# Holding back two gathers of old key blocks until the second attention group's rows have landed, in a one-core four-layer kernel

## What is computed

```
k_blocks = k_blocks.at[blk, :, off, :].set(k)     # 64 x 32 new keys go into the cache
v_blocks = v_blocks.at[blk, :, off, :].set(v)
k_all = k_blocks[block_tables] ...                # rows of each entry's window
scores = einsum(qg, k_all) * SCALE                # masked to a window of 128 positions
p = softmax(scores)
o = einsum(p, v_all) ; out = einsum(o, Wo)
```

## Time and profile before

| what | us |
|---|---|
| runs before | 958.57, 965.36, 964.55; median 964.55 |
| the profiled execution | 957.4, of it span 955.3 |
| attention, start of the keys of the first and of the last entry | 459.08 and 597.5 |

### The profile page before, as it was taken

How to read it: one execution, slowest core, us unless ns; L and a number is a source line. 1 busy time by engine, 2 the same in 40 slices (tenths; PEclk the granted TensorE clock), 3 DMA queues, 4 the chain that set the end, 5 groups by cost and what they waited for, 6 DMA issues and landing times.

```text
span 955.3 us, 16539 instructions
## 1 busy us (share of the span) xinstructions
PE 832.4 (87%) x5239; PEld 674.2 (71%) x5239; DVE 567.7 (59%) x1659; ACT 347.7 (36%) x1007; POOL 381.1 (40%) x405
## 2 busy tenths in 40 slices
PE   1999998976899998785489799979979979999997
PEld 1787776754798997674378687877447747777786
DVE  5656888655587886289288799451553434444343
ACT  3333443433233332112277788402442222221311
POOL 7300436367566676766545540000175003434000
PEclk9999999996999999898599999959999979999999
DMA  9226111787977551924888876000523003331232
GB/s 353 67 89 177 47 44 63 295 252 215 247 212 229 159 139 38 348 78 121 159 166 172 160 168 218 2 1 1 187 101 123 24 17 93 104 104 57 89 82 94
DMA packets 68179, 126.43 MB, mean 132 GB/s; under 512 B 20224, under 2 KB 50265, under 8 KB 65455
## 3 DMA queue, kind: packets, MB, share of 16 engines
q1 hardware_dynamic: 46783, 75.49, 26.3%
q0 software_dynamic: 20800, 47.76, 18.1%
q10 hardware_dynamic: 512, 2.13, 1.0%
HBM read 87.39 MB, written 43.30 MB: 137 GB/s over the span
## 4 chain that ended last, share of the span: by engine, by line
PE 59%; DMA 13%; DVE 10%; issue 5%; SPq 5%; ACT 4%; POOL 3%; DVEq 0%; POOLq 0%; ACTq 0%
PE ps L470 18%; PE ps L807 10%; PE ps L838 7%; SPq L1097 3%; PE ps L817 3%; DMA early<-newblk,new_i 2%; DMA early<-early 2%; PE ps L2277 2%; DMA big<-mid 2%; PE ps L828 2%; DMA mid<-sent_d 2%; PE ps L2514 2%; PE ps L2293 2%; PE ps L2559 1%; POOL sent_d L909 1%
## 5 line engine op out<-in xcount | busy, mean ns | idle before, releaser
L909 POOL DMA_INDIRECT sent_d<-mid,slot_i x88 | 98.3, 1117 | 111.1 <-DVE mid L629 65.2
L851 ACT ACTIVATE early<-ps 128x256 f32<-128x256 f32 x134 | 51.5, 384 | 175.0 <-PE ps L817 173.3
L838 PE MATMUL ps<-early 96*128 (+1 forms) x346 | 97.5, 382 | 0.2
L869 DVE TENSOR_TENSOR early<-early,ps 128x96 f32<-128x96 f32 (+1 forms) x134 | 37.3, 278 | 96.0 <-ACT early L857 80.1
L900 POOL DMA_INDIRECT back_d<-early,mid x78 | 77.1, 989 | 35.1 <-issue 29.9
L504 DVE TENSOR_TENSOR hidl<-work,hidh 128x512 fp32r<-128x512 f32 (+1 forms) x56 | 38.8, 693 | 84.4 <-ACT hidh L497 84.4
L807 PE MATMUL ps<-big,early 128*128 x380 | 81.2, 337 | 3.6 <-issue 2.0
L900 POOL DMA_INDIRECT back_d<-big,mid x39 | 38.4, 985 | 112.6 <-DVE big L883 106.7
L510 ACT ACTIVATE work<-ps 128x512 f32<-128x512 f32 (+1 forms) x56 | 33.4, 596 | 136.4 <-PE ps L470 136.2
L807 PEld LDWEIGHTS ps<-big,early 128*128 128x128 f32 x380 | 68.8, 196 | 10.4 <-issue 5.4
L807 PE MATMUL ps<-early 128*128 x156 | 56.0, 482 | 4.6 <-ACT early L851 4.4
(11 more groups left out here) (440 smaller groups left out, 2094.3 us busy)
## 6 DMA issues: line engine op xcount, KB each, us to landing
mid<-sent_d SPq DMA_DIRECT2D x117, 130.0 KB
big<-back_d SPq DMA_DIRECT2D x8, 512.0 KB
mid<-back_d SPq DMA_DIRECT2D x8, 512.0 KB, 6.4
early<-back_d SPq DMA_DIRECT2D x16, 256.0 KB, 3.1
early<-in_w SPq DMA_DIRECT2D x3, 1024.0 KB, 11.9
big<-in_gate SPq DMA_DIRECT2D x1, 3072.0 KB, 10.7
big<-in_up SPq DMA_DIRECT2D x1, 3072.0 KB, 15.8
early<-in_gu SPq DMA_DIRECT2D x1, 2816.0 KB, 10.6
```

What stands on the lines that cost most here:

```text
L838: last = nc.tensor.matmul(ps[:, 6 + j % 2, 0:D], L.hTb[j % len(L.hTb)][0:f1 - f0, h * P:(h + 1) * P], L.down[0:f1 - f0, h, bass.ds(owners[ ...
L851: nc.scalar.activation(L.yTb[b % ring_y], ps[:, b % 2, 0:2 * P], ACT.Copy).then_inc(s["turn_sb"], 1)
L869: nc.vector.tensor_tensor(L.hb[j % ring_h], L.sgb[j % 2], ps[:, 2 + j % 2, F:2 * F], ALU.mult)\
L909: nc.gpsimd.indirect_dma_start(out=sent_d, out_offset=bass.IndirectOffsetOnAxis(ap=L.slot_i[:, i:i + 1], axis=0), in_=L.rows[c][:, t, n, : ...
```

## The change

In the part written out by hand, GpSimd issues the gather of group 4 not between the turns of groups 1 and 2 but behind the turn of group 2, and it waits there until SyncE's half of the turn of group 1 has landed. The turn of group 3 moves up, ahead of the gather of group 5. All transfers stay the same.

```diff
             turn_rows(1)
-            old_rows(4)
             pool.wait_ge(s["qkv_end"], 1)
             nc.gpsimd.memset(pickw, 0.0).then_inc(s["qzero"], 1)
             turn_rows(2)
+            pool.wait_ge(s["into1"], turned(1))
+            old_rows(4)
+            turn_rows(3)
             old_rows(5)
             new_rows(4)
             old_rows(6)
-            turn_rows(3)
             new_rows(5)
             old_rows(7)
             for g in range(6, NT):
```

## The result

The changed kernel takes 965.95 us (median of 20 runs, 960.50 to 971.63) against 961.81 us of the kernel before (20 runs, 957.35 to 967.37). The ratio is 1.004, with a 95% interval of 1.0021 to 1.006: about 4 us or 0.4% slower, as forecast, though less than the 1% that the prediction took as what a measurement can tell from no change. The execution profiled after took 961.96 us.

What follows compares the result with a forecast made beforehand. The prediction took the chain of turns and new rows up to group 11's landing as the bound. Group 1's gain 0, rows' delay +4.0, rest 0, on the 964.55 us median: 968.5 us, range 957.5 to 978.

Steps and rivals of the forecast that it cites:

- What bounds the kernel: Attention: a chain of turns and new rows up to group 11's landing; TensorE's 7.58 us wait before group 1 off it.
- The rows of group 1: SyncE's last issue to landing: 5 us instead of 11.5, TensorE starting group 1 some 6.5 us sooner, worth nothing by itself.
- The gather of group 4: GpSimd: issued 10.7 us later, 8 us from it to new rows 4, which go 7.5 us later.
- New rows 6: GpSimd: the gather of group 6 ends last instead of the turn of group 2; 3.5 us delay on this path.
- SyncE's turns: SyncE's queue: turn 4 at 487.1 instead of 479.53; turn 6 late by 3.5 to 5.8 us, taken as 4.0.
- From there to group 11: Later rounds of the loop: the delay is handed on at the same 33 us a round, no change counted.
- signs of being wrong: Group 1 landing after 472, new rows 6 issued before 484.17, or group 11 starting before 561 or after 571.
- the hidden delay: Rival: SyncE's pauses of 2.47 and 1.75 us and later ones swallow the delay; 964.5 us, chance 0.25.
- The earlier loop: Rival: sooner turns of groups 1 and 2 and quick gathers send new rows 6 3.5 us sooner; 960 us, chance 0.15.
- The serial chain on the slow side: Rival at GpSimd's new wait and SyncE's turn 4: new rows 4 13.7 us late; 978.3 us, chance 0.15.

Runs made afterwards that it cites:

- e5: The changed kernel once more, unedited, as a second profile; ratio 1.0057 to the kernel before.
- e10: Against the changed kernel: gather of group 4 held only until SyncE's half of the turn of group 0 has landed; ratio 0.999 to the kernel before.
- e2: Against the changed kernel: the new wait before the gather of group 4 removed, the changed order kept; ratio 0.9988 to the kernel before.
- e3: Against the changed kernel: gather of group 4 held until the turn of group 2 has landed, instead of group 1; ratio 1.0095 to the kernel before.
- e4: Against the kernel before: gathers of groups 4 and 5 issued early, right behind that of group 3; ratio 1.0061.
- e9: Against e4: gathers of groups 6 and 7 put behind new rows 4 and 5, turn 3 ahead of them; ratio 1.0049 to the kernel before.
- e1: The kernel before once more, unedited, as a second profile of it; ratio 1.0001.

## Why the prediction was right

The forecast was +4.0 us; the measured difference is 4.1, and 5.5 in e5. The steps, one by one, with the prediction's clock times turned into times from SyncE's first turn (minus 451.25):

- *What bounds the kernel.* The long wait before group 1 isn't on the path. This held: e10 takes 5.5 us off the start of group 1 and shows no gain.
- *The rows of group 1.* I took 5 us from SyncE's last issue to the landing; it is 475.07 - 470.39 = 4.7, and 3.7 in e5. Keys of group 1 were forecast at 17.6 and stand at 17.3 and 17.8. By the rule of the Trainium skill ("DMA: Bandwidth & Descriptors", "Queues, rings and completion order") that each DMA engine takes turns between its queues, the prediction would have put them near 15.7; the trace agrees with its direction, since they came sooner once the gathers were gone, and not with that bound. TensorE's wait there is 3.17 us, not about 1.
- *The gather of group 4.* Forecast at 17.9, measured 18.2 and 18.6. I took 8 us from it to new rows 4; it was 8.7 and 9.7. The landing alone took 7.88 in the chain, and 8.86 in e5's. New rows 4 were forecast at 25.9 and came at 26.9 and 28.3. The fit of the Trainium skill (same page, "Anatomy of one DMA") gave an estimate of 3.7 us; no gather of this stretch came near it.
- *New rows 6.* This step was undersized. I forecast 36.5, 3.5 us late; it was 38.5 and 39.9, so 5.5 and 6.9 us late on the mean of before, 33.0. The mechanism was right: the slack over gather 6 is used up and the gather is the releaser. What was undersized is mostly not the transfers. From gather 6 to new rows 6 it is 10.3 us in both profiles (485.95 to 496.21 in the first), of which the landing takes 9.4, near my 9; the rest is the pause of over 0.8 us between a landing and the instruction that waited for it. I took GpSimd's gap as 0.3 us, which is what lies between two issues when nothing is waited for, and behind the landing of gather 4 I took none. The pause comes three times on this path, behind turn 1, gather 4 and gather 6, and makes up nearly all of the 2.0 us missing in the first profile; in e5 it is 1.9 of 3.4, and the slower landing of gather 4 is most of the rest.
- *SyncE's turns.* Turn 4 was forecast at 35.9 and came at 35.0 and 36.4. I took 10.0 us to it from new rows 4, as before, and it took 8.1 and 8.0. Turn 6, for which I took +4.0 between 3.5 and 5.8, was late by 6.7 and 6.8 us. It didn't wait for new rows 6: turns 4 and 5 end at 492.78 + 14.47 = 507.25, and turn 6 begins at 507.35. So SyncE's own issues set it, and turns 4 and 5 took longer (14.47, in e5 14.26) than the 12.92 of before, where I had reckoned with less.
- *From there to group 11.* I counted no change here. In the first profile that was wrong: SyncE issues turns 6 and 7 in 12.12 us instead of 15.58, group 4 starts only 1.8 us late although turn 4 was issued 6.8 us late, and group 11, for which I forecast 113.75, starts at 110.0, just where it did before. In e5 the delay goes on to the end: group 11 starts at 112.9 and the last keys 6.9 us late on the mean of before. The medians differ by only 4.1, less than the 6.7 at turn 6, so something of the delay is made up on the way in most executions; how much, two such unlike profiles don't show. So an undersized delay and a recovery that I had left out worked against each other. The direction, the gather of group 6 as releaser and the size of several us came from the mechanism; that the sum came so close to the median is luck.

Of the signs of being wrong none came up once 6.49 us are taken off: group 1 landed at 468.6, new rows 6 went at 489.7, and group 11 started at 561.25, hardly above the 561 that I had set as its lower bound.

The rivals: the hidden delay is excluded for the changed kernel by both intervals, but the mechanism exists. Within 0.3% either way it swallows the first 7 us by which gather 4 is put off (e2, e10). The earlier loop didn't come, since new rows 5 and 6 waited for their gathers instead of the turns. The serial chain on the slow side is the same mechanism pushed further: e3 puts new rows 4 some 15 us late and costs 0.95%. I had priced it without slack, 13.7 us for new rows 4 that come 13.7 us late; with slack they cost less.

Three things stay open: whether e4 really loses another 3 us or so behind the first turn while e9 doesn't, as each has one profile; where in the loop the slack of about 3 us at new rows 6 lies; and whether the later start of the first turn in three profiles (457.7 to 462.7, against 451.0 to 456.3) is chance. If it isn't, part of the 4.1 us lies ahead of the edited instructions, and the marks here don't see it.

## What to carry to other kernels

When a wait is removed from an engine that later waits again for the same supply, look for the last wait, not the longest: starting the group behind the longest one 6.7 us sooner bought nothing here. A transfer on a shared queue can be put off at no cost only up to the slack of what stands behind it, and everything behind it on that queue moves with it, so find the slack first; here one that let go 4 us sooner (e10) kept most of the gain at group 1 at no cost that could be measured. And where executions scatter as much as the effect, count times from a mark just ahead of the change and take at least two profiles of each kernel.

## What the runs showed that I had not expected

With two gathers of 44 rows issued early on GpSimd's queue, SyncE's first turn, which waits for the small gather issued behind them, came 2.7 (e4) and 5.7 us (e9) later after that gather's issue, although the DMA engines were only 0.57 busy there in the kernel before (e1). And the same kernel, profiled twice, put the last keys of the attention at 145.6 and 152.1, although everything up to group 4 repeated within 1.5 us.
